# Graph attention edges on one core: one of 32 gathered tiles is copied row by row by SyncE and ScalarE

## The reference

```
feat = (h @ W).reshape(n, H, F)
el = sum(feat * al, -1);  er = sum(feat * ar, -1)
e = leaky_relu(el[src] + er[dst], 0.2)
m = segment_max(e, dst);  ex = exp(e - m[dst])
a = ex / segment_sum(ex, dst)[dst]
out = segment_sum(feat[src] * a, dst) + b
out = elu(out)
```

## Time and profile before

| | |
|---|---|
| time, median of 3 runs | 7253.21 us (7250.66 to 7256.73) |
| span of the profiled execution | 7256.0 us |
| VectorE busy | 5474.7 us (75%) |
| GpSimd busy | 5227.7 us (72%) |
| TensorE / ScalarE busy | 2303.6 us (32%) / 2204.3 us (30%) |
| moved by DMA | 1467.62 MB, mean 202 GB/s |

### The profile page before, as it was taken

How to read it: one execution, slowest core, us unless ns; L and a number is a source line. 1 busy time by engine, 2 the same in 40 slices (tenths; PEclk the granted TensorE clock), 3 DMA queues, 4 the chain that set the end, 5 groups by cost and what they waited for, 6 DMA issues and landing times. The chain is left out here.

```text
span 7256.0 us, 61622 instructions
## 1 busy us (share of the span) xinstructions
PE 2303.6 (32%) x10543; PEld 1546.4 (21%) x10543; DVE 5474.7 (75%) x9449; ACT 2204.3 (30%) x5437; POOL 5227.7 (72%) x5323
## 2 busy tenths in 40 slices
PE   4688888888888573000000000026000000000000
PEld 3455555555555462000000000014000000000000
DVE  7799999999999575666676767664566666666668
ACT  2688888888888341000000000001000000000001
POOL 4677777777776636777777777757777777777775
PEclk8899999999999797555555555568555555555555
DMA  7666676666666567676666666654567676766667
GB/s 227 189 203 204 204 205 204 204 204 203 204 204 188 139 164 186 208 221 211 218 213 215 216 213 218 210 155 102 179 209 223 208 223 208 221 210 219 212 211 237
DMA packets 822248, 1467.62 MB, mean 202 GB/s; under 512 B 216345, under 2 KB 552862, under 8 KB 821660
## 3 DMA queue, kind: packets, MB, share of 16 engines
q0 software_dynamic: 250192, 671.13, 34.7%
q1 hardware_dynamic: 571980, 795.64, 32.2%
HBM read 754.27 MB, written 713.36 MB: 202 GB/s over the span
## 5 line engine op out<-in xcount | busy, mean ns | idle before, releaser
L1774 POOL DMA_INDIRECT gb_g<-table,ix_g x3126 | 2976.1, 952 | 954.5 <-issue 949.2
L665 POOL DMA_INDIRECT gb<-table,ix x1563 | 1615.9, 1034 | 494.9 <-issue 471.6
L1855 DVE SCALAR_TENSOR_TENSOR gb_g<-gb_g,same_g,wv 128x256 f32<-128x256 f32 x3028 | 1452.1, 480 | 93.6
L1050 PE MATMUL pm<-ident,tl 128*4 128x128 f32 x2 | 0.7, 372 | 4035.4 <-DMA tl<-sums 4035.4
L1787 ACT ACTIVATE ww<-ee 128x132 f32<-128x132 f32 x98 | 27.8, 284 | 3643.1 <-DVE ee L1832 3643.1
L1843 DVE TENSOR_TENSOR wv<-gb_g,ww 128x1024 f32<-128x1024 f32 (+1 forms) x782 | 954.8, 1221 | 0.0
L696 PE MATMUL po<-msg,sel 128*128 128x256 f32 x3144 | 858.1, 420 | 148.2 <-DVE msg L808 143.9
L1823 DVE TENSOR_TENSOR ee<-gb_g,held 128x128 f32<-128x128 f32 (+1 forms) x98 | 37.4, 381 | 1110.1 <-DMA gb_g<-table,ix_g 1110.1
L1050 PEld LDWEIGHTS pm<-ident,tl 128*4 128x4 f32 x2 | 0.2, 81 | 4036.2 <-DMA tl<-sums 4036.2
L696 PEld LDWEIGHTS po<-msg,sel 128*128 128x128 f32 x3144 | 614.1, 206 | 384.0 <-DVE msg L808 237.3
L688 PE MATMUL pt<-m,r 64*128 64x256 f32 x3136 | 461.9, 412 | 228.0 <-DVE msg L849 225.5
(11 more groups left out here) (282 smaller groups left out, 4326.2 us busy)
## 6 DMA issues: line engine op xcount, KB each, us to landing
sums<-gb_g SPq DMA_DIRECT2D x780, 528.0 KB, 3.5
sums<-ost SPq DMA_DIRECT2D x393, 512.0 KB, 3.2
gb_g<-table,ix_g POOLq DMA_INDIRECT x3126, 3.1
gb<-table,ix POOLq DMA_INDIRECT x1563
table<-f SPq DMA_DIRECT2D x48, 520.0 KB, 6.8
x<-in_x SPq DMA_DIRECT2D x50, 256.0 KB, 3.9
at<-in_rbf SPq DMA_DIRECT2D x100, 128.0 KB
hT_d<-hT SPq DMA_DIRECT2D x49, 256.0 KB, 3.4
```

Source lines behind the costliest of these rows:

```text
L665: eng.indirect_dma_start(out=gb[:, g, j, :, :].rearrange("p a c -> p (a c)"), out_offset=None, in_=q.table0[:, :], in_offset=bass.Indirect ...
L1774: eng.indirect_dma_start(out=gb[:, p, j, 0:FR], out_offset=None, in_=q.table1[:, :], in_offset=bass.IndirectOffsetOnAxis(ap=ix[:, p, j:j + ...
L1855: ins = eng.scalar_tensor_tensor(rows[:, t, 0:D], behind, same[:, t:t + 1], wv[k % 2][:, j, :], ALU.mult, ALU.add)
```

## The change

In a group of 32 tiles the tile COPIED = LAST - 1 = 26 is no longer gathered by GpSimd, which now issues 31 gathers (26 in the last group). Its 128 rows are copied one at a time by plain DMAs, each with its row number in a register: rows 0 to 63 by SyncE, rows 64 to 127 by ScalarE. The numbers come from a new input, `src_copied`, with 128 numbers of a group in a row; `numbers` fetches 32 of them from device memory into registers. ScalarE copies the rows of group s+1 behind its work for group s. SyncE does it in eight parts of eight rows, part k ahead of the store k of group s. The rows of group 0 are copied ahead of the loop, on SyncE ahead of the constant fills. VectorE waits for 31 gathers and for both sets of rows.

```
+COPIED = LAST - 1 if LAST > 1 else SBT - 1
+BY_SP = 64
...
-        s_g = [Signal(q.sem(nm(f"g{p}")), per=SBT, inc=16) for p in range(B)]
+        s_g = [Signal(q.sem(nm(f"g{p}")), per=SBT - 1, inc=16) for p in range(B)]
+        s_rs = [Signal(q.sem(nm(f"rs{p}")), per=BY_SP, inc=16) for p in range(B)]
+        s_ra = [Signal(q.sem(nm(f"ra{p}")), per=P - BY_SP, inc=16) for p in range(B)]
...
+        def numbers(eng, s, r0, r1):
+            _, values = nc.values_load_multi_w_load_instructions(a["src_copied"][bass.ds(s, 1), r0:r1], engines=[eng.engine], min_val=0, max_val=N - 1,
+                                                                 skip_runtime_bounds_check_because="they are numbers of nodes")
+            return values
+
+        def row(eng, p, r, number, signal):
+            eng.dma_start(gb[r:r + 1, p, COPIED, 0:FR], q.table1[bass.ds(number, 1), :]).then_inc(signal.sem, 16)
...
             @block.sync
...
+                def copies(s, i, p, k):
+                    step = BY_SP // NQ
+                    if k == 0:
+                        if p == B - 1:
+                            eng.wait_ge(s_held, H)
+                        eng.wait_ge(s_st[p].sem, s_st[p].at(i, back=1))
+                        eng.nop(nofuse=True)
+                        eng.wait_ge(s_sum.sem, s_sum.at(s, 1, back=2))
+                        eng.nop(nofuse=True)
+                    if k * step % 32 == 0:
+                        wanted[:] = numbers(eng, s, k * step, min(k * step + 32, BY_SP))
+                    for r in range(k * step, (k + 1) * step):
+                        row(eng, p, r, wanted[r % 32], s_rs[p])
...
-                    eng.wait_ge(s_seg.sem, s_seg.at(s))
                     for k, ts in enumerate(quads(last)):
+                        if not last:
+                            copies(i * B + (p + 1), i + (p + 1) // B, (p + 1) % B, k)
+                        if k == 0:
+                            eng.wait_ge(s_seg.sem, s_seg.at(s))
+                            eng.nop(nofuse=True)
                         eng.wait_ge(s_sum.sem, s_sum.at(s, k + 1))
...
                 eng.dma_start(ch, q.er_start[0:EC, :].rearrange("(p e) h -> p (e h)", p=P)).then_inc(s_ch, 16)
+                for k in range(NQ):
+                    copies(0, 0, 0, k)
...
             @block.gpsimd
...
                     for j in range(tiles):
+                        if j == COPIED:
+                            continue
...
             @block.scalar
...
+                def copies(s, i, p):
+                    if p == B - 1:
+                        eng.wait_ge(s_held, H)
+                    eng.wait_ge(s_st[p].sem, s_st[p].at(i, back=1))
+                    eng.nop(nofuse=True)
+                    eng.wait_ge(s_sum.sem, s_sum.at(s, 1, back=2))
+                    eng.nop(nofuse=True)
+                    for r0 in range(BY_SP, P, 32):
+                        wanted = numbers(eng, s, r0, min(r0 + 32, P))
+                        for x, number in enumerate(wanted):
+                            row(eng, p, r0 + x, number, s_ra[p])
...
+                copies(0, 0, 0)
                 with eng.Fori(0, SB // B) as i:
                     for p in range(B):
                         body(i * B + p, p)
+                        copies(i * B + (p + 1), i + (p + 1) // B, (p + 1) % B)
...
             @block.vector
...
-                    eng.wait_ge(s_g[p].sem, s_g[p].at(i, tiles))
+                    eng.wait_ge(s_g[p].sem, s_g[p].at(i, tiles - 1))
+                    eng.wait_ge(s_rs[p].sem, s_rs[p].at(i))
+                    eng.wait_ge(s_ra[p].sem, s_ra[p].at(i))
```

More of the change, by code:

```diff
@@ L1732, in indices @@
                     eng.dma_start(ix[:, p, :], a["src_chunks"].rearrange("p (s t) -> s p t", t=SBT)[s, :, :]).then_inc(s_ix[p].sem, 16)
+                def copies(s, i, p, k):
[11 more added lines that the diff above has]
+                        row(eng, p, r, wanted[r % 32], s_rs[p])
+                wanted = []
                 def body(s, i, p, last):
@@ L1898 @@
         "src_chunks": _np.concatenate([srcp[:EC].reshape(P, CE), _np.zeros((P, CH - CE + 2 * SBT), src.dtype)], axis=1),
+        "src_copied": _np.concatenate([srcp[:EC].reshape(P, CE), _np.zeros((P, CH - CE), src.dtype)], axis=1)[:, COPIED::SBT].T,
         "dst_rows": dstp.reshape(T, P),
```

## The result

| | before | after |
|---|---|---|
| median | 7251.93 us (7247.94 to 7256.73, 4 runs) | 8112.18 us (8105.18 to 8117.60, 4 runs) |
| span of the profiled execution | 7256.0 us | 8115.9 us |

The changed kernel takes 1.118 times the time, 95% interval 1.117 to 1.120: 860 us slower. The forecast was 8500 us in a range of 7700 to 9400.

A forecast was written before the change was run, and what follows sets the result against it. GpSimd's 32 gathers were taken to bound each group at 40.0 us, ScalarE's row copies to raise that to 52.2. The profiled 7256 + 1171 for longer periods + 72 for pass starts = 8499, say 8500 us, range 7700 to 9400.

The forecast's parts named there:

- Forecast: Main case, attention edges: row copies on ScalarE set a 52.2 us period, 8500 us; chance 0.62, own range 8050 to 8950.
- A row, 0.48 us: Row copies on SyncE and ScalarE: register operation, MOVE, DMA and gaps take 0.48 us a row, 30.8 us for 64.
- A fetch, 7.3 us: Loading row numbers into registers on SyncE and ScalarE: 0.215 us a number, 7.3 us for 34; the largest unknown.
- Which path is the later: Between VectorE's first gathered-row operations of successive groups: ScalarE's path 52.2 us, SyncE's 49.7, so ScalarE's sets the period.
- A store, 0.6 us: SyncE's stores between row copies: about 0.6 us each, six on its path, 3.6 us.
- The landing, 1.7 us: End of both engines' paths: the last row copy lands 1.7 us later, as a small load does.
- The loop's return: Branch back in the longer loops: 32 returns at 1.7 us, an estimated 54 us, left at nothing since no row priced it.
- The start of a pass: Group 0's rows ahead of SyncE's constant fills: first period 89.6 us, +72 us over two passes.
- Numbers that come together: Rival on fetches into registers: 2.2 us each, SyncE the bound, 7740 us; chance 0.17.
- Dearer rows: Rival on row copies: 0.615 us a row gives about 9350 us, 0.79 us over 10,300; chance 0.10.
- Cheap issue, faster: Rival on the 64 issues an engine: 0.36 us a row, GpSimd stays the bound at 38.8 us, 7160 us; chance 0.11.

The follow-up runs named there:

- kernel of two of three groups: Changed kernel with the tile copied row by row only in two of three groups (middle and last buffer), copies spread over all; 7183.5 us, 0.9895 of the kernel before.
- one of three groups: Changed kernel with the tile copied row by row only in one of three groups (middle buffer); 9714.8 us, 1.128 of the kernel before, which took 8609 us there.

## Why the prediction was right

**The direction and the mechanism held; the engine named as the bound did not.** VectorE's wait for gathers became a wait for rows, GpSimd waits for buffers, in both passes, and the rest of the program kept its time. But SyncE's path ends last, not ScalarE's. "Forecast" of the four cases is the one that happened: 8112 lies in its own range of 8050 to 8950.

**The time was over by 388 us of 8500; of the forecast rise of 1243 us 69% came.** A part of the nearness is luck. The path that was named as the bound, ScalarE's, was forecast 7.7 us too long (52.2 us, and 44.5 measured); by it alone the time would be some 7740 us (an estimate: 7253 + 96 x 4.5 and some 60 for the starts), below the forecast's own range. SyncE's path, which took over, was forecast at 49.7 us and measured at 47.8, with errors that in part cancel. Term by term:

- *A row, 0.48 us.* SyncE's takes 0.44 us in the mean, ScalarE's 0.41: the DMA instruction 228 and 213 ns in place of the 287 of the single element, the register operation 37 in place of 46. The gaps of 0.04 were about right. One in 12 of SyncE's takes 0.35 to 0.9 us, which lifts the DMA's mean to 253 ns.
- *A fetch, 7.3 us.* It takes 4.9 us: 1.1 for the address and 3.8 for the numbers. That they come one at a time is right; the price of one, taken as the middle of ends a factor of 55 apart, was the mis-sized term. In the kernel of two of three groups the loads of 8, 20, 24 and 32 numbers take 1.02, 2.40, 2.9 and 3.9 us: 0.12 us a number, where 0.215 was taken. The address of two words takes 1.1 us, 0.9 more than that slope gives for two numbers. The 200 ns per register of the Trainium skill (Runtime: NRT & Kernel Launch, "Instruction fetch mechanics") is closer, but also too high: by it 32 numbers are 6.4 us.
- *Which path is the later.* This step failed. The prediction put ScalarE's at 52.2 us and SyncE's at 49.7. Measured, ScalarE's is 5.0 (start) + 36.8 (fetches 10.0, rows 26.8) + 2.7 = 44.5 us; SyncE's is 10.4 (first row behind the first store) + 34.7 (56 rows, six stores, a fetch) + 2.7 (landing) = 47.8 us. ScalarE has two fetches on its path and SyncE one, so the dear fetch had been charged twice to the one and once to the other. That alone makes them even (47.4 and 47.3 us with 4.9 us a fetch in the prediction's sums); ScalarE's cheaper rows and SyncE's dearer stores turn the order round.
- *A store, 0.6 us.* From the last of eight rows to the next eight 0.76 us pass (median), six times on the path.
- *The landing, 1.7 us.* 2.7 us, from the last row's issue to VectorE's start.
- *The loop's return, left at nothing.* SyncE stands 3.9 us (median) behind its branch at L1787 once in three groups and ScalarE 3.7 us behind its own, where both stood 0.2 us in the kernel before. In those groups SyncE's first row behind the first store starts 12.2 us after L1875 and not 10.4 (medians), and the period is 49.3 us and not 47.8. Over a round that is the 0.5 us a group between 47.8 and the 48.3 measured (four groups of five lie between 47.4 and 49.9). That the return is what costs it is read from the trace and was not shown by an experiment in the usual condition. The prediction had an estimate of 54 us for it and left it out; 0.5 us in 96 groups are 48.
- *The start of a pass.* The second L1875 stands 75.1 us after the first, forecast 89.6: fetches are cheaper, and L1785 holds SyncE 33.9 us and not 39.9. SyncE copies ahead of the fills, as forecast: first fetch to last row 43.2 us (2814.4 to 2857.6), where 45.4 were forecast. The first fetch of a pass is dear, 11.6 us in both.

**The rivals.** Numbers that come together: refuted by the loads of four sizes. Dearer rows: refuted, 0.44 us is under 0.48. Cheap issue, faster: its place was right and its price out of reach, since it asked for 56 rows and a fetch in 23.4 us of SyncE, which take 30 us without the stores. The rule of the Trainium skill (DMA: Bandwidth & Descriptors, "Issuing engines are not separate DMA queues") that the sequencer's time is usually small beside the DMA holds for one row: 0.44 us with its register work, and 2.7 us to the landing. It misleads for a run of rows: 64 issues in a row are 28 us of a 48 us group.

That the loss does not come of rows as such is shown by the kernel of two of three groups. That it is one of quantity beside each group is argued from the sum of SyncE's stream, since that kernel has its rows in other places too. That one fetch of 5.1 us lies on SyncE's path is read from the rows alone.

## What to carry to other kernels

Work that is taken from a bound engine and given to the sequencers of two others has to fit into the time the bound leaves, on each of them by itself and with everything that stands in its stream: here 128 rows an engine in three groups, spread over all three, fit and 192 did not, and the same idea went from 12% slower to 1% faster. Price register work as real work: a row is three instructions and 0.41 to 0.44 us, a fetch of 32 numbers 4.9 us. Where a path ends last on one of two engines, count how often the least certain price stands on each before saying which.

## What the runs showed of the hardware

- A fetch of numbers from device memory into registers took 0.12 us a number (8 to 32 numbers), and that of a two-word address 1.1 us.
- A DMA of one row of 1040 bytes with its number in a register took 213 ns (ScalarE) and 228 ns (SyncE) of the issuing engine, less than the 332 ns of a store of 128 rows.
- The return of SyncE's loop took 0.23 us with a round of 136 instructions (kernel before), 0.24 with 348 (one of three groups, in the other condition), 2.8 with 565 and 3.9 with 750 (medians). That instructions are fetched again there fits the queue q14, of kind "instruction": 48, 133, 395 and 523 packets. The kernel with the loops written out moved 368.
- In the sessions in which the kernel before took 19 to 20% longer, SyncE and ScalarE ran in bursts at 0.70 us an instruction, and GpSimd did not. There the kernels with rows took 13 to 38% more than the kernel before; in the usual condition the one of two of three groups took 1% less. No kernel with rows was run in both.
